# Grouped self attention of layer 0: the values become the weights of the product and stream four heads at once, with the normalisation on GpSimd ahead of it

## The chip, the cores and the metric

The program runs on one core of a Trainium2 chip. A core has five engines with queues of their own: TensorE (matmuls, with weight loads that overlap them), VectorE, ScalarE, GpSimd and SyncE, which here issues most DMAs. They meet only through semaphores. The metric is the time on the device of one execution, in microseconds; lower is better. In the rows of the profile PE is TensorE's matmul, PEld its weight load, DVE is VectorE, ACT is ScalarE, POOL is GpSimd, SP is SyncE.

## The reference

Two decoder layers over x of shape (8, 112, 512): B = 8 batches, T = 112 tokens, D = 512 features. Each layer has a self attention, a cross attention and a feed-forward block. Only one piece is touched, the attention inside `_L0_ffn_ref`: 32 query heads of 64 features share 8 key/value heads, 4 query heads each, with a causal mask.

```python
q = (h @ wq).reshape(B, S, NHEADS, HEAD_DIM)      # 32 heads of 64
k = (h @ wk).reshape(B, S, KVHEADS, HEAD_DIM)     # 8 heads of 64
v = (h @ wv).reshape(B, S, KVHEADS, HEAD_DIM)
q, k = _rope(q, k)
k, v = jnp.repeat(k, g, axis=2), jnp.repeat(v, g, axis=2)      # g = 4
scores = jnp.einsum('bqhd,bkhd->bhqk', q, k) / np.float32(np.sqrt(HEAD_DIM))
scores = jnp.where(causal[None, None], scores, jnp.float32(-1e+30))
attn = jax.nn.softmax(scores, -1)
o = jnp.einsum('bhqk,bkhd->bqhd', attn, v).reshape(B, S, NHEADS * HEAD_DIM)
x = x + o @ wo
h = _rms(x, ff_ln_w)
```

## The kernel before

The kernel is a chain of segments with one engine barrier between them. The one that matters is "self2". Its parts are written as generators, one for each engine; `attention_order` gives one list of turns, and `Segment.play` advances the named part by one turn on every engine. So each engine has a fixed order of instructions, and only semaphores tie the engines.

The attention part ("a", class `SelfAttentionPart`, L1466 to L1659) works on items. An item is one key/value head of one batch with its group of 4 query heads; two items (W = 2) make a step, so a batch has 4 steps and the segment 32, plus 2 to drain. Each step x has two turns, A and B:

- TensorE, A: transposes of the probabilities of pair x-2 (L1578, 8 of them, into the banks `t_banks`), then the scores of pair x (L1589, 8 matmuls with 64 rows; two items lie in the upper and the lower 64 rows). B: the value products of pair x-2 (L1602, 8 matmuls, the transposed probabilities as weights, 128 columns of the values streaming).
- VectorE, A: for each item the mask is added (L1618), reading the scores from PSUM and writing `p`; then the maximum of each row (L1622). B: for pair x-2 the reciprocal of the row sum (L1632) and the product into `o` (L1640). The row sum comes out of the value product itself: the value tile has a 65th column of ones for each head.
- GpSimd, A: the maximum is subtracted (L1565).
- ScalarE, A: copies of the transposes from PSUM (L1652). B: the exponential (L1656).

Here x-2 is counted on TensorE and ScalarE in steps, as LT = 2 and LE = 2. TensorE's transposes wait for `exp_done` of their item, the value products for `pt_ready`, the scores for `mask_done` of two items before.

The output part ("o", class `OutNormPart`, L2037 to L2285) works batch by batch, with 4 units of 512 columns: it turns a unit of `o` on TensorE (L2278, 4 transposes), ScalarE and VectorE split it into a high and a low half (L2127, L2179, tiles `oT_hi`, `oT_lo`), and TensorE multiplies by Wo (L2246, L2248, L2250, 12 matmuls of 512 columns for a unit). When a batch has its 4 units, VectorE adds and takes the moments (L2186 to L2151, the turn called ADD), GpSimd takes the power (L2118), VectorE scales (L2213, the turn NORM), and two turns later the result is turned (L2260) and split (L2130, L2167). With `gap=1.5` there are about two turns of "o" for three of "a": over four steps they stand after turn A of each step and once more after turn B of the third.

The part "w" (`WeightSplitPart`) splits Wo into halves in eight turns near the start (L2023 on ScalarE, L2031 on VectorE). `FirstBatchPart` (L2878) belongs to the segment before, "p2": it loads queries, keys and values of batch 0 ahead of time, the values in pieces of 64 into rows of 65, behind a memset of ones. `laid_out` is run on the host and only lays out the inputs.

The class `JointAttentionPart` of layer 1 (L1847 to L1998) is not changed, but the prediction reads prices there: its GpSimd normalises `p` before the transposes (L1920), and its value product has the values as weights and streams 448 columns (L1953).

Of the kernel before, what the change touches and what calls it, by code (L numbers as in the profile page):

```python
# [183 lines left out]
def reuse(eng, sem, value):  # L184

    if not isinstance(value, int) or value > 0:
        eng.wait_ge(sem, value)
# [1472 lines left out]


class CrossAttentionPart:

# [1214 lines left out]
class FirstBatchPart:  # L2878


    def __init__(self, g, name, p, loads, ones=None):
        landed, ones_set = g.sem(f"{name}_landed"), g.sem(f"{name}_ones_set")

        def sync(sp):
            yield
            n = 0
            for items, pairs in zip(((21,), (28,), (35,)), loads):
                sp.wait_ge(p.mm_done, TT)
                for i in items:
                    if i < 35:  # L2890
                        sp.wait_ge(p.t_stored[i % 3], 16 * (i // 3 + 1))
                    else:
                        sp.wait_ge(p.v_stored[0], 16)
                        if ones is not None:
                            sp.wait_ge(ones_set, 1)
                for to, src in pairs:
                    sp.dma_start(to, src).then_inc(landed, 16)
                    n += 16
                yield
            sp.wait_ge(landed, n)  # L2900

        def gpsimd(pool):
            yield
            if ones is not None:
                pool.wait_ge(p.mm_done, TT)
                pool.memset(ones, 1.0).then_inc(ones_set, 1)
            yield

        g.part(name, sync=sync, gpsimd=gpsimd)

# [442 lines left out]
def decoder(nc, ins, out, blocks=range(6), debug_x=None):  # L3353

    with ExitStack() as ctx:
# [8 lines left out]
        def tokens_of(b):  # L3364
            return slice(b * T, (b + 1) * T)

        def own_qkv(dh, heads, scale, *banks_and_mask):

            return (dh, None, lambda b: q_all[:, tokens_of(b)], lambda b: k_all[:, tokens_of(b)], lambda b: v_all[tokens_of(b), :],
                    heads, scale, *banks_and_mask)  # L3370

        def head_qkv(p):
# [63 lines left out]
        with hold_h0:  # L3436
            last_values = LastStores(core, hold_h0, "x2_last_values", [128, D])
            with ExitStack() as inner:
                cos_t = inner.enter_context(nc.sbuf_tensor("f0_cos", [128, TT, 2, 32], F32))
                sin_t = inner.enter_context(nc.sbuf_tensor("f0_sin", [128, TT, 2, 32], F32))  # L3440
                with Segment(core, "p2") as g:
# [4 lines left out]
                    k2 = first_hi[:, :, :].bitcast(F32).rearrange("p k d -> p (k d)")[:, 0:8 * T].rearrange("p (u c t) -> p u c t", u=2, c=4)  # L3446
                    v2 = first_lo[0:T, :, :].bitcast(F32).rearrange("p k d -> p (k d)")[:, 0:2 * (8 * 65 + 128)].rearrange("p (u e) -> p u e", u=2)
                    f = FirstBatchPart(g, "f", p, [
                        [(q2[0], q_all[:, tokens_of(0)].rearrange("(c p) t -> p c t", p=128))],
                        [(k2[:, 0, :, :], k_all[:, tokens_of(0)].rearrange("(c p) t -> p c t", p=128))],  # L3450
                        [(v2[:, 0, 0:8 * 65].rearrange("p (h e) -> p h e", e=65)[:, :, 0:64], v_all[tokens_of(0), :].rearrange("t (h d) -> t h d", d=64))]],
                        ones=v2)
                    order = ["p"] * 4 + ["p", "t", "t"] * (t.steps // 2)
                    g.run(f.placed(order + ["t"] * (t.steps - order.count("t")) + ["p"] * (p.steps - order.count("p"))))
            with Segment(core, "self2") as g:
                wo = [g.sb(f"wo_{part}", [128, 16, D], F32R) for part in ("hi", "lo")]
                a = SelfAttentionPart(g, "a", *own_qkv(64, 32, 0.125, (0, 1), (2, 3), (4, 5), "causal", ALU.add), tiles=(q2, k2, v2))
                w = WeightSplitPart(g, "w", "L0_ffn_wo", *wo)
# [100 lines left out]
def laid_out(inputs):  # L3559
# [18 lines left out]
    def pieces(w):  # L3578

        return rows_first(w).reshape(128, B, -1).transpose(1, 0, 2)  # L3580
# [13 lines left out]
    ins["L0_ffn_wk"], ins["L0_ffn_wv"] = rows_first(a["L0_ffn_wk"]), rows_first(a["L0_ffn_wv"])  # L3594
    ins["L0_ffn_wo"] = pieces(a["L0_ffn_wo"])
    ins["L0_ffn_wg"] = rows_first(a["L0_ffn_wg"])
# [48 lines left out]
```

## Time and profile before

| what | us |
|---|---|
| median of 3 runs | 2788.76 (2788.07 to 2790.92) |
| the profiled execution, its device time | 2790.01 |
| the profiled execution, its span | 2788.1 |
| TensorE busy in the span | 2570.0 (92%) |
| VectorE, ScalarE, GpSimd busy | 1694.7, 1132.2, 896.6 |
| segment "self2", first scores to last value product of it | 745.3 to about 972 |

The span runs from the first to the last instruction of the program. Busy time is a union over instructions; matmuls overlap, so a TensorE that is busy all the time may still have a little room. The granted clock is TensorE's, as a share of 2.4 GHz; its two levels are 1.00 and 0.50. In a timeline each line has start, duration (of a merged run, from the first start to the last end), engine, line of the program, tiles, count, and in brackets the idle time before it with what ended it.

### The profile page before, as it was taken

What the parts mean: (1) busy time and instruction counts of PE and PEld (TensorE: products, weight loads), DVE (VectorE), ACT (ScalarE), POOL (GpSimd) and SP (SyncE); (2) the same over time, 40 slices, a digit from 0 to 9 for tenths busy, and PEclk for the clock granted to TensorE, in tenths of its full rate; (3) what the DMA queues carried; (4) which work ended last, traced back from release to release, by engine and by line L of the source; (5) the groups of instructions that cost most, each with busy time, mean ns of one, the idle gap of its engine ahead of it and who ended that gap; (6) DMA issues with size and microseconds to landing.
All of it is one profiled execution on the core that took longest, in us unless ns stands there. A gap on an engine that the chain in (4) does not pass through costs nothing. (4 is left out here: it accounts for less than half of the span.)

```text
span 2788.1 us, 48182 instructions
## 1 busy us (share of the span) xinstructions
PE 2570.0 (92%) x14667; PEld 2065.4 (74%) x14668; DVE 1694.7 (61%) x3341; ACT 1132.2 (41%) x2434; POOL 896.6 (32%) x919
## 2 busy tenths in 40 slices
PE   8999799979899989799997898998999999899998
PEld 7888677768688877678875777774665678788887
DVE  4537757769776657567675566864434325666664
ACT  2113255533343324445453133755555522444443
POOL 3213100014332225423223200753333322345555
PEclk9999999999899979899998898999999989999999
DMA  5553122125532045388774432444222031566664
GB/s 188 154 144 99 31 92 63 59 66 154 162 104 64 15 142 172 123 235 224 193 213 120 112 73 70 131 132 149 73 64 73 22 128 55 154 163 161 162 153 81
DMA packets 289277, 332.87 MB, mean 119 GB/s; under 512 B 147445, under 2 KB 202693, under 8 KB 287312
## 3 DMA queue, kind: packets, MB, share of 16 engines
q1 hardware_dynamic: 217904, 252.57, 29.1%
q0 software_dynamic: 20640, 51.74, 9.6%
q10 hardware_dynamic: 50560, 26.34, 3.3%
q8 instruction: 99, 1.62, 0.2%
q14 instruction: 74, 0.61, 0.1%
HBM read 233.86 MB, written 96.72 MB: 119 GB/s over the span
## 5 line engine op out<-in xcount | busy, mean ns | idle before, releaser
L898 PE MATMUL e_psum<-e_up_hi,hT_hi 128*128 x672 | 245.2, 365 | 21.5 <-DVE hT_lo L867 14.6
L900 PE MATMUL e_psum<-e_up_hi,hT_lo 128*128 x672 | 236.7, 352 | 0.0
L899 PE MATMUL e_psum<-e_up_lo,hT_hi 128*128 x672 | 236.4, 352 | 0.0
L1920 POOL TENSOR_TENSOR joint_a_p<-joint_a_p,joint_a_rinv 112x487 f32<-112x487 f32 x128 | 125.2, 999 | 195.9 <-DVE joint_a_rinv L1966 195.5
L1565 POOL TENSOR_TENSOR self_a_p<-self_a_p,self_a_mx 112x448 f32<-112x448 f32 x96 | 96.0, 1000 | 205.2 <-DVE self_a_mx L1622 205.2
L898 PEld LDWEIGHTS e_psum<-e_up_hi,hT_hi 128*128 128x128 f32 x672 | 127.5, 190 | 43.6 <-issue 32.3
L1971 DVE TENSOR_REDUCE joint_a_mx<-joint_psum 112x1 f32<-112x487 f32 x128 | 85.0, 664 | 121.5 <-PE joint_psum L1941 121.2
L794 ACT ACTIVATE e_gate<-e_psum 128x352 f32<-128x352 f32 (+1 forms) x86 | 44.4, 516 | 256.4 <-PE e_psum L900 252.1
L873 DVE TENSOR_TENSOR hT_lo<-e_psum,hT_hi 128x256 fp32r<-128x256 f32 (+2 forms) x138 | 55.7, 435 | 142.1 <-ACT hT_hi L812 139.0
L1656 ACT ACTIVATE self_a_p<-self_a_p 112x448 f32<-112x448 f32 x128 | 71.6, 575 | 164.8 <-POOL self_a_p L1565 113.8
L900 PEld LDWEIGHTS e_psum<-e_up_hi,hT_lo 128*128 128x128 f32 x672 | 127.5, 190 | 11.5
L899 PEld LDWEIGHTS e_psum<-e_up_lo,hT_hi 128*128 128x128 f32 x672 | 127.7, 190 | 9.7
L1209 POOL TENSOR_TENSOR p_p_z<-p_p_straight,p_p_crossed 128x512 f32<-128x512 f32 x70 | 98.4, 1406 | 112.1 <-DVE p_p_crossed L1191 112.1
L828 DVE TENSOR_TENSOR e_up_lo<-e_up_raw,e_up_hi 128x1024 f32 (+3 forms) x128 | 128.0, 1051 | 3.2 <-issue 3.0
L766 POOL DMA_INDIRECT out<-e_y,e_back x51 | 123.2, 2416 | 17.3 <-issue 17.3
L847 DVE SCALAR_TENSOR_TENSOR e_act_raw<-e_gate,e_rows,e_psum 128x352 f32<-128x352 f32 (+1 forms) x86 | 55.4, 645 | 118.3 <-ACT e_gate L794 115.9
L898 PE MATMUL e_psum<-e_dn_hi,hT_hi 128*128 (+1 forms) x285 | 121.3, 426 | 1.0 <-issue 0.3
L1941 PE MATMUL joint_psum<-x_first,x_q 128*112 128x487 f32 x256 | 117.8, 582 | 1.8 <-PEq L89 1.7
L752 POOL TENSOR_TENSOR e_held<-e_zeros 1x1 f32<-1x1 f32 x90 | 19.7, 218 | 308.2 <-DVE e_idx L862 308.2
L142 PE MATMUL p_psum<-p_p_w_hi,hT_hi 128*128 128x512 f32 x280 | 115.5, 412 | 1.9 <-DVE p_p_w_lo L1175 1.9
L1994 ACT ACTIVATE joint_a_p<-joint_psum,joint_a_neg 112x487 f32<-112x487 f32 x128 | 85.4, 667 | 75.8 <-DVE joint_a_neg L1973 72.5
L781 ACT ACTIVATE e_up_hi<-e_up_raw 128x1024 f32 (+3 forms) x128 | 107.8, 923 | 15.1 <-PEq L89 15.1
(561 smaller groups left out, 7484.6 us busy)
## 6 DMA issues: line engine op xcount, KB each, us to landing
e_up_raw<-in_L_ffn_w SPq DMA_DIRECT2D x64, 512.0 KB, 4.8
e_up_raw<-in_L_ffn_w SPq DMA_DIRECT2D x64, 352.0 KB
e_dn_raw<-in_L_ffn_w SPq DMA_DIRECT2D x16, 1024.0 KB, 14.2
q_all<-p_p_t_stage ACTq DMA_DIRECT2D x56, 256.0 KB
e_dn_raw<-in_L_ffn_w SPq DMA_DIRECT2D x16, 512.0 KB
x_q<-q_all SPq DMA_DIRECT2D x8, 896.0 KB
v_ctx<-front_c_v_stage SPq DMA_DIRECT2D x24, 250.0 KB
x_others<-k_ctx SPq DMA_DIRECT2D x8, 750.0 KB, 4.6
```

The costliest lines, as they stand in the source:

```text
L142: last = pe.matmul(out, a, b, start=(k == 0 and i == 0), stop=(k == n_k - 1 and i == len(pairs) - 1))
L766: pool.indirect_dma_start(out=acc, out_offset=bass.IndirectOffsetOnAxis(ap=back[:, v, :], axis=0), in_=y[:, v, :], in_offset=None, compute ...
L781: act.activation(up_hi[:, bass.ds(slot * KC + k, 1), :], up_raw[:, k:k + 1, :], ACT.Copy).then_inc(up_hi_ready, 1)
L828: dve.tensor_tensor(up_lo[:, bass.ds(slot * KC + k, 1), :], up_raw[:, k:k + 1, :], up_hi[:, bass.ds(slot * KC + k, 1), :].bitcast(F32), AL ...
L898: pe.matmul(out, lhs[0], rhs[0], start=k == 0, stop=False)
L899: pe.matmul(out, lhs[0], rhs[1], start=False, stop=False)
L900: return pe.matmul(out, lhs[1], rhs[0], start=False, stop=k == n_k - 1)
L1209: both = pool.tensor_tensor(z[:, r, :], straight[:, r, :], crossed[:, r, :], ALU.add)
L1565: pool.tensor_tensor(p[:, i % RING, :, :], p[:, i % RING, :, :], mx[:, i % RING, :].unsqueeze(2).to_broadcast([T, group, T]), ALU.subtract ...
L1920: pool.tensor_tensor(p[:, r, :], p[:, r, :], rinv[:, r:r + 1].to_broadcast([T, S]), ALU.mult).then_inc(p_ready, 1)
L1941: pe.matmul(ps[0:T, s_banks[i % N_S], 0:S], q[:, b % 2, h, :], k[:, b % 2, h // group, :], start=True, stop=True).then_inc(s_done, 1)
L1994: act.activation(p[:, r, :], ps[0:T, s_banks[i % N_S], 0:S], ACT.Exp, bias=neg[:, r, :], scale=scale, accum_out=rsum[:, r:r + 1]).then_inc ...
```

## The change

A new class `GroupedSelfAttentionPart` takes the place of `SelfAttentionPart` in this one segment; the other two self attentions keep the old one. The steps, the two turns, the scores, the mask, the maximum, the subtraction, the exponential and the transposes stay. What differs:

- The value product. The weights are now the values of one key/value head (112 rows, 64 columns), and the transposed probabilities of the item's four heads stream as one block of 448 columns. The two items of a pair write the upper and the lower 64 partitions of one PSUM bank. 8 matmuls a pair become 2.
- Its result is feature-major. The output part reads it from PSUM with `ot_view` (`turned = True`), so `o`, the product into it (L1640) and the transposes L2278 are gone. Wo's rows are permuted on the host to the new order of heads.
- The row sum can't come from a column of ones any more. VectorE sums the rows of `p` of pair x-1 (L1794, a reduction for each item) in turn B, and takes one reciprocal for both items (L1798). GpSimd multiplies `p` by it in turn B (L1735). The transposes of pair x-2 wait for that product (`p_ready`), not for the exponential.
- The ring of transposed tiles `pt` has 4 places instead of 2; the values are loaded as plain rows of 512; `FirstBatchPart` loses the memset of ones.

Line numbers from L1655 on are those of the changed program here.

```diff
+        def gpsimd(pool):
...
+                for i in pair(step):
+                    pool.wait_ge(mx_ready, i + 1)
+                    pool.tensor_tensor(p[:, i % RING, :, :], p[:, i % RING, :, :], mx[...], ALU.subtract).then_inc(less_ready, 1)
+                yield
+                for i in pair(step, 1):
+                    pool.wait_ge(rinv_ready, i // W + 1)
+                    pool.tensor_tensor(p[:, i % RING, :, :], p[:, i % RING, :, :], rinv[...], ALU.mult).then_inc(p_ready, 1)
+                yield
+        def tensor(pe):
...
+                for i in pair(step, LT):
+                    pe.wait_ge(p_ready, i + 1)
+                    reuse(pe, pt_ready, i - N_T + 1)
+                    for j in range(group):
+                        last = pe.transpose(ps[0:T, t_banks[i % N_T], j * T:(j + 1) * T], p[:, i % RING, j, :], core.ident[0:T, 0:T])
+                    last.then_inc(t_done, 1)
...                                  # then the scores of the step, as before
+                yield
+                both = pair(step, LT)
+                if both:
...
+                    pe.wait_ge(pt_ready, both[-1] + 1)
+                    reuse(pe, self.o_used, at - N_O + 1)
+                    for i in both:
+                        n = i % n_items
+                        last = pe.matmul(ps[rows_of(i), o_banks[at % N_O], 0:group * T], v[:, b % 2, n * dh:(n + 1) * dh],
+                                         pt[:, i % PT, :, :].rearrange("p h t -> p (h t)"), start=True, stop=True)
+                    last.then_inc(pv_done, 1)
+        def vector(dve):
...                                  # mask and maximum of the step's pair, as before
+                yield
+                before = pair(step, 1)
+                for i in before:
+                    dve.wait_ge(exp_done, i + 1)
+                    dve.tensor_reduce(rsum[:, i % RING, :], p[:, i % RING, :, :], AX.X, ALU.add).then_inc(sum_ready, 1)
+                if before:
+                    at = before[0] % RING
+                    dve.wait_ge(sum_ready, before[-1] + 1)
+                    dve.reciprocal(rinv[:, at:at + W, :], rsum[:, at:at + W, :]).then_inc(rinv_ready, 1)
...
-                a = SelfAttentionPart(g, "a", *own_qkv(64, 32, 0.125, (0, 1), (2, 3), (4, 5), "causal", ALU.add), tiles=(q2, k2, v2))
+                a = GroupedSelfAttentionPart(g, "a", lambda b: q_all[:, tokens_of(b)], lambda b: k_all[:, tokens_of(b)], lambda b: v_all[tokens_of(b), :],
+                                             0.125, "causal", (0, 1), (2, 3), (4, 5), (q2, k2, v2))
...
-    ins["L0_ffn_wo"] = pieces(a["L0_ffn_wo"])
+    ins["L0_ffn_wo"] = pieces(a["L0_ffn_wo"].reshape(4, 2, 4, 64, D).transpose(0, 2, 1, 3, 4).reshape(4 * D, D))
```

How this stands on the engines. VectorE before, in the middle of the segment, from the second item's mask of one step on:

```order
L1618 TENSOR_TENSOR self_a_p<-self_psum,self_a_mask 112x448
L1622 TENSOR_REDUCE self_a_mx<-self_a_p 112x4
L2179 TENSOR_TENSOR self_o_oT_lo<-self_psum,self_o_oT_hi 128x448
L1632 RECIPROCAL self_a_rinv<-self_psum 112x4
L1640 TENSOR_TENSOR self_a_o<-self_psum,self_a_rinv 112x256
```

VectorE now, at the same place, to the end of the step (a step that also has the output part's split of the turned result):

```order
L1786 TENSOR_TENSOR self_a_p<-self_psum,self_a_mask 112x448
L1789 TENSOR_REDUCE self_a_mx<-self_a_p 112x4
L2336 TENSOR_TENSOR self_o_oT_lo<-self_psum,self_o_oT_hi 128x448
L1794 TENSOR_REDUCE self_a_rsum<-self_a_p 112x4 x2
L1798 RECIPROCAL self_a_rinv<-self_a_rsum 112x8
L2324 TENSOR_TENSOR hT_lo<-self_psum,hT_hi 128x4x112
```

The row sums of the pair before stand behind the mask and the maximum of this pair and behind the output part's turn; the reciprocal and the product of the finished pair are gone.

TensorE before, from the end of one output projection over the next step:

```order
L2248 MATMUL self_psum<-self_wo_lo,self_o_oT_hi 112x512
L2250 MATMUL self_psum<-self_wo_hi,self_o_oT_lo 112x512
L2278 MATMUL self_psum<-ident,self_a_o 128x112 x4
L1602 MATMUL self_psum<-x_first_lo,self_a_pt 112x128 x8
L1578 MATMUL self_psum<-ident,self_a_p 112x112 x8
L1589 MATMUL self_psum<-x_first_hi,x_wp_lo 112x112 x8
```

TensorE now, at the same place (L1747 are the transposes, L1758 the scores, L1772 the value products):

```order
L2405 MATMUL self_psum<-self_wo_lo,self_o_oT_hi 112x512
L2407 MATMUL self_psum<-self_wo_hi,self_o_oT_lo 112x512
L1772 MATMUL self_psum<-self_a_pt,x_first_lo 64x448 x2
L1747 MATMUL self_psum<-ident,self_a_p 112x112 x8
L1758 MATMUL self_psum<-x_first_hi,x_wp_lo 112x112 x8
```

The transposes still stand directly ahead of the scores; the turning of `o` is gone and the value products are 2 instead of 8.

## Rows read from the trace of the kernel before

**Rows 1.** Stretches of the segment: us, busy time by engine, PEclk, DMA share, GB/s.
```profile
745.30:788.00 42.70, 37.55 (x294) 32.43 (x294) 32.92 (x60) 23.53 (x37) 16.80 (x15) 0.82 0.61 174
788.00:954.30 166.30, 166.30 (x1369) 142.38 (x1368) 118.55 (x272) 62.90 (x129) 50.71 (x54) 1.00 0.19 51
```

**Rows 2.** Timeline of TensorE over one batch: start, duration, line, operands, count.
```profile
849.42 0.93 PE L1578 MATMUL self_psum<-ident,self_a_p 112*112 112x112 f32 x8
850.28 1.04 PE L1589 MATMUL self_psum<-x_first_hi,x_wp_hi 64*112 64x112 f32 x16
851.25 0.60 PE L2278 MATMUL self_psum<-ident,self_a_o 112*128 112x112 f32 x4
851.69 1.91 PE L1602 MATMUL self_psum<-x_first_lo,self_a_pt 112*112 112x128 f32 x16
853.44 0.93 PE L1578 MATMUL self_psum<-ident,self_a_p 112*112 112x112 f32 x8
854.30 1.04 PE L1589 MATMUL self_psum<-x_first_hi,x_wp_hi 64*112 64x112 f32 x16
...
861.15 1.04 PE L1589 MATMUL self_psum<-x_first_hi,x_wp_hi 64*112 64x112 f32 x16
...
871.17 1.04 PE L1589 MATMUL self_psum<-x_first_hi,x_wp_hi 64*112 64x112 f32 x16
```

**Rows 3.** Groups by line and shape, 788 to 954.3: busy, mean ns, idle before.
```profile
L1622 DVE TENSOR_REDUCE self_a_mx<-self_a_p 112x4 f32<-112x448 f32 x48 | 29.8, 621 | 1.6
L2213 DVE SCALAR_TENSOR_TENSOR self_w_raw<-h,self_o_rstd,self_o_w_row 112x512 f32<-112x512 f32 x6 | 4.5, 742 | 0.0
```

**Rows 4.** Timelines at the segment's start, TensorE, VectorE, GpSimd; low clock.
```profile
745.32 1.84 PE L1589 MATMUL self_psum<-x_first_hi,x_wp_hi 64*112 64x112 f32 x16 [5.16 <-PEq L89]
749.10 1.84 PE L1589 MATMUL self_psum<-x_first_hi,x_wp_hi 64*112 64x112 f32 x16 [1.95 <-DVE self_a_p L1618]
747.23 0.62 DVE L1618 TENSOR_TENSOR self_a_p<-self_psum,self_a_mask 112x448 f32<-112x448 f32 x1 [3.10 <-PE self_psum L1589]
747.89 0.62 DVE L1622 TENSOR_REDUCE self_a_mx<-self_a_p 112x4 f32<-112x448 f32 x1
748.43 0.61 DVE L1618 TENSOR_TENSOR self_a_p<-self_psum,self_a_mask 112x448 f32<-112x448 f32 x1
749.08 0.62 DVE L1622 TENSOR_REDUCE self_a_mx<-self_a_p 112x4 f32<-112x448 f32 x1
748.59 0.93 POOL L1565 TENSOR_TENSOR self_a_p<-self_a_p,self_a_mx 112x448 f32<-112x448 f32 x1 [2.76 <-DVE self_a_mx L1622]
```

**Rows 5.** Timeline of VectorE, an ADD turn of the output part.
```profile
961.05 0.68 DVE L2186 TENSOR_TENSOR h<-self_psum,h 112x512 f32<-112x512 f32 x1
...
963.64 0.61 DVE L2179 TENSOR_TENSOR self_o_oT_lo<-self_psum,self_o_oT_hi 128x448 fp32r<-128x448 f32 x1
964.17 0.17 DVE L1632 RECIPROCAL self_a_rinv<-self_psum 112x4 f32<-112x4 f32 x1
```

**Rows 6.** Timeline of the joint stage: value product, products on GpSimd, transposes.
```profile
1901.17 2.90 PE L1953 MATMUL joint_psum<-joint_a_pt,x_v 125*128 125x448 f32 x7 [2.01 <-ACT joint_a_pt L1988]
...
1909.42 1.96 POOL L1920 TENSOR_TENSOR joint_a_p<-joint_a_p,joint_a_rinv 112x487 f32<-112x487 f32 x2 [5.91 <-DVE joint_a_rinv L1966]
1910.47 2.12 PE L1933 MATMUL joint_psum<-ident,joint_a_p 112*125 112x112 f32 x8 [3.56 <-POOL joint_a_p L1920]
```

**Rows 7.** A wait of TensorE in the first self attention, and the clock of stretches.
```profile
340.15 1.01 PE L2260 MATMUL self_psum<-ident,self_p_w_raw 112*128 112x112 f32 x4 [5.83 <-DVE self_p_w_raw L2222]
340.20:347.20 7.00, 5.71 (x17) 4.84 (x18) 1.37 (x2) 0.54 (x1) 0.00 (x0) 0.50 0.00 0
745.30:760.20 14.90, 11.86 (x79) 10.78 (x80) 8.64 (x17) 6.65 (x11) 5.69 (x7) 0.50 0.72 192
```

**Rows 8.** Timeline of VectorE and GpSimd at a splitting step of Wo.
```profile
763.98 1.22 DVE L2031 TENSOR_TENSOR self_wo_lo<-self_w_raw,self_wo_hi 128x1024 fp32r<-128x1024 f32 x1
764.14 1.84 POOL L1565 TENSOR_TENSOR self_a_p<-self_a_p,self_a_mx 112x448 f32<-112x448 f32 x1 [0.25 <-DVE self_a_mx L1622]
```

**Rows 9.** DMA issues around the start of the segment: KB each, us to landing.
```profile
x_first_lo<-v_all SPq DMA_DIRECT2D x2, 224.0 KB, 4.5
```

More of the change, by code:

```diff
@@ L2878, with __init__ @@
 class FirstBatchPart:
-    def __init__(self, g, name, p, loads, ones=None):
-        landed, ones_set = g.sem(f"{name}_landed"), g.sem(f"{name}_ones_set")
+    def __init__(self, g, name, p, loads):
+        landed = g.sem(f"{name}_landed")
         def sync(sp):
@@ L2893, in sync @@
                         sp.wait_ge(p.v_stored[0], 16)
-                        if ones is not None:
-                            sp.wait_ge(ones_set, 1)
                 for to, src in pairs:
@@ L2900, in sync @@
             sp.wait_ge(landed, n)
[L2902 to L2909, printed above, removed]
+        g.part(name, sync=sync)
     def placed(self, order):
@@ L3365, in tokens_of @@
             return slice(b * T, (b + 1) * T)
-        def own_qkv(dh, heads, scale, *banks_and_mask):
-            return (dh, None, lambda b: q_all[:, tokens_of(b)], lambda b: k_all[:, tokens_of(b)], lambda b: v_all[tokens_of(b), :],
-                    heads, scale, *banks_and_mask)
         def head_qkv(p):
@@ L3446, in decoder @@
                     k2 = first_hi[:, :, :].bitcast(F32).rearrange("p k d -> p (k d)")[:, 0:8 * T].rearrange("p (u c t) -> p u c t", u=2, c=4)
-                    v2 = first_lo[0:T, :, :].bitcast(F32).rearrange("p k d -> p (k d)")[:, 0:2 * (8 * 65 + 128)].rearrange("p (u e) -> p u e", u=2)
+                    v2 = first_lo[0:T, :, :].bitcast(F32).rearrange("p k d -> p (k d)")[:, 0:2 * D].rearrange("p (u e) -> p u e", u=2)
                     f = FirstBatchPart(g, "f", p, [
@@ L3450, in decoder @@
                         [(k2[:, 0, :, :], k_all[:, tokens_of(0)].rearrange("(c p) t -> p c t", p=128))],
-                        [(v2[:, 0, 0:8 * 65].rearrange("p (h e) -> p h e", e=65)[:, :, 0:64], v_all[tokens_of(0), :].rearrange("t (h d) -> t h d", d=64))]],
-                        ones=v2)
+                        [(v2[:, 0, :], v_all[tokens_of(0), :])]])
                     order = ["p"] * 4 + ["p", "t", "t"] * (t.steps // 2)
```

105 lines of the change are left out of this document (added).

## The prediction, made before the changed kernel ran

> **What bounds the kernel now.** I read four views. The stretches first: inside the segment "self2" the middle 166.3 us have TensorE busy for all 166.30 us at granted clock 1.00, with VectorE at 118.55 and GpSimd at 50.71 [rows 1]; no stage outside this segment is touched. The timeline of TensorE next: the segment is 32 steps (8 batches x 4), each two items of four heads; from one score burst (L1589) to the next pass 4.02, 6.85, 10.02 and, in the fourth step as in the second, 6.85 us, 27.7 us for a batch [rows 2], and no idle time is noted between. Then the groups by line, for the price of one instruction [rows 3], and last the timelines at the segment's start, where engines do wait and the delay of each hand-over can be read [rows 4 to 6]. So today TensorE's own work sets the time, and everything else hides under it.
>
> **What TensorE loses in work.** For a pair of items the value products take 16 passes, 1.75 us from 851.69 to 853.44; the turning of the output (L2278) takes 0.44 us, 851.25 to 851.69 [rows 2]. After the change the pair's value product has four passes of 448 columns. By the 16 passes just named a pass costs 109 ns for 128 columns, so 0.38 for 448; the joint stage has passes of just this length, seven in 2.90 us with the last one's tail [rows 6], which agrees. One behind the other four make 1.52 us; if the two halves of the array run side by side, as the scores' two items do (16 passes of 112 columns in 0.97 us, 850.28 to 851.25, against 16 of 128 columns in 1.75 [rows 2]), three lengths or 1.14 us. L2278 goes. TensorE's work for a batch is then 27.7 - 4 x (0.42 + 0.23) = 25.1 us, or 23.6 with the halves side by side. The Trainium skill, "TensorEngine Tiling (Array Packing)", section "Theoretical Speedup", allows up to 2x for operands of at most 64 columns; by it the pair would cost 0.75 and the batch some 22 us. No row shows column halves at work, and the forecast below doesn't hang on it, since TensorE will no longer be what is waited for.
>
> **What the change adds, and where it lies.** Each item gets a row sum on VectorE and a normalising product on GpSimd before its transposes. The order that decides is this. In step x VectorE has mask and maximum of pair x (these need the scores of x), then the output part's work, then the row sums and reciprocal of pair x-1. GpSimd multiplies pair x-1 after that, TensorE turns pair x-1 after that, and only behind those transposes stand the scores of x+1. Before the change the transposes of x-1 waited for the exponential alone, long past. Now every step is one ring: scores x, VectorE, GpSimd, transposes x-1, scores x+1, and nothing in the ring can run ahead. I price it from the end of one score burst to the end of the next:
> - hand-over to VectorE 0.05 (the burst ends at 745.32 + 1.84 = 747.16, the mask starts at 747.23, at the low clock) [rows 4];
> - mask, maximum, mask, maximum: 747.23 to 749.08 + 0.62 = 749.70, 2.47 [rows 4];
> - one oT_lo of the output part, which stands between A and B turns in the order: 963.64 to 964.17, 0.53 [rows 5];
> - two row sums. They are not in the trace; the nearest row is the maximum over the same tile, 621 ns [rows 3], which advances the queue by about 0.54 (747.89 to 748.43) as other queued work does: 1.08. Bounds 1.0 to 1.3;
> - reciprocal 0.17 [rows 5] and its wait 0.03 (maximum behind its mask, 747.85 to 747.89 [rows 4]): 0.20; hand-over to GpSimd 0.08 (747.89 + 0.62 to 748.59) [rows 4];
> - two products over 112x448. The nearest row is the subtraction of the same shape, 0.93 undisturbed (748.59 [rows 4]); two queued ones overlap slightly (two of 487 columns take 1.96 [rows 6]): 1.82. Bounds 1.8 to 2.0;
> - GpSimd to TensorE 0.05 (first product 1909.42 + 1.00, transposes at 1910.47 [rows 6]), the second item's four transposes and the burst 1.52 (the eight start at 849.42, so the last four near 849.80; the burst ends at 850.28 + 1.04 = 851.32) [rows 2].
>
> Sum **7.80 us** for a plain step. In the step in which the output part adds a batch (ADD), seven more VectorE instructions stand ahead of the row sums: 961.05 to 963.64, 2.59 [rows 5], making 10.39. In the next one (NORM) one more of 742 ns [rows 3], 0.66 net: 8.46. The step with two output projections has TensorE as the slower: 10.02 - 0.4 - 0.23 to 0.61 = about 9.2. A batch: 7.80 + 10.39 + 8.46 + 9.2 = **35.85 us** against 27.73, +8.12. For the 6 batches of the middle stretch [rows 1]: **+48.7 us**.
>
> **The clock.** In the ADD step TensorE has only the value product (1.1 to 1.5) after the scores and then waits: the first product on GpSimd ends 0.05 + 2.47 + 2.59 + 0.53 + 1.08 + 0.20 + 0.08 + 0.93 later, 7.9, so some 6.5 us idle. The trace has one gap of that kind in the earlier self attention, 5.83 us ahead of 340.15, and the granted clock after it is 0.50 (1.2 instead of 2.4 GHz) for the 7.0 us from 340.20 [rows 7]. Four transposes and a burst at the low clock cost 0.32 + 0.80 more (burst 1.84 instead of 1.04 [rows 2, 4], four transposes 0.75 instead of 0.43), 1.2 us; the projection that follows slows down too, but hides under the ring (7.5 us of cover). 6 x 1.2 = **+7.2 us**. The Trainium skill, "TensorE: Matmul & The Clock Gate", section "HAM oscillation — how this bites in real kernels", says that waits between bursts make each burst start throttled; the row at 340.20 agrees. Without such a fall the total is 7 us less, and a fall that outlasts the projection is a rival below.
>
> **Head, tail, edge.** The first seven steps take 42.7 us now [rows 1], partly at the low clock. After: 3.8 (unchanged, bound by the mask, see the wait at 749.10 [rows 4]), then 7.80 - 0.53 + 1.2 = 8.5, then 9.4, three steps of 11.05, then 11. The last ones contain splitting steps of Wo: one ahead of the row sums (1.22 - 0.08 = 1.14) and one that keeps GpSimd from starting, as at 764.14 where a subtraction takes 1.84 instead of 0.93 while L2031 runs (+0.91) [rows 8]. Sum 65.9, **+23** (15 to 28). The tail exchanges a longer ring for less TensorE work, +1. Ahead of the segment the load of the values (4.5 us to land now, in pieces of 64 numbers [rows 9]) gets long pieces and loses its wait for the memset of ones: 0 to -2, I take -1. The permuted Wo and the value loads of later batches have the same bytes and lie under a queue that nobody waits for.
>
> Sum: 48.7 + 7.2 + 23 + 1 - 1 = **+79 us**. The profiled execution took 2790.0 us with a span of 2788.1, within 2 us of the median of 2788.76, so I add to the median: **2868 us**.
>
> **Rivals.**
> - *TensorE stays the bound.* If the ring were not closed (VectorE reaching the row sums of x-1 before it has to wait for scores x), TensorE's saving would be paid out: 0.65 to 1.0 us for each of 32 steps, 21 to 33 us, 2756 to 2768. It decides at 25 us a batch; the ring would have to shrink by 10. For it: TensorE's share of 1.00 and the idle quarter of VectorE. Against it: the order on VectorE, word for word. 7%.
> - *The low clock holds.* If the clock stays at 0.50 from the ADD step through the NORM step, projection (5.3), value product (2.3 to 3), transposes and scores (3.6) make the NORM step about 11.7 instead of 8.5 and cost some 3 more in the next: 7.4 instead of 1.2 a batch, +37 us, 2905. For it: from 745.3 to 760.2 the clock stayed at 0.50 with TensorE busy for 11.86 of 14.90 us [rows 7]. 15%.
> - *A shorter ring.* Overlap that I don't see (products of GpSimd running beside the sums, ADD work finding holes): 2 us less in each of 24 steps, 2800 to 2840. 10%.
> - *The halves don't run side by side.* Then only the step with two projections grows, by 0.2: no case of its own.
>
> **The numbers.** The forecast, a closed ring with one clock fall a batch, gets 66%, the low clock 15%, the shorter ring 10%, TensorE as the bound 7%, no change 2%. Own bounds of the ring (sums, products, head, no fall) give 2849 to 2885; the range takes in the shorter ring's upper edge and the low clock: **2840 to 2906**. A measurement of this kernel can tell 0.2% (6 us). Faster 7%, same 2%, slower 91%.
>
> **What would show it.** In the profile after: the mask's starts 7.8, 10.4, 8.5 and 9.2 apart instead of 4.0 to 10.0; TensorE waiting for GpSimd's product (L1735) at the transposes in three steps of four, 1.5 to 6.5 us; VectorE waiting for scores; TensorE's busy share in the middle near 70%; granted clock below 1.00 behind the ADD steps; row sums of 0.62 and products of 0.93. Wrong it would be if TensorE showed no gaps there, if the row sums of x-1 were seen ahead of the mask of x, or if GpSimd's product took far less than the subtraction.

## The result, and the profile after

The changed kernel takes **2888.08 us** (median of 4 runs, 2884.75 to 2891.72) against 2788.64 (2788.07 to 2790.92, 4 runs) for the kernel before: ratio 1.0354, 95% interval 1.0341 to 1.0367. It is slower by 99 us; 79 were forecast, in a range of 51 to 117.

The profile page of the changed kernel: span, busy time by engine, the granted clock in forty slices, and the group of the transposes with the wait ahead of it.

```profile
span 2890.0 us, 47097 instructions
...
PE 2579.8 (89%) x14155; PEld 2027.9 (70%) x14156; DVE 1701.4 (59%) x3309; ACT 1137.4 (39%) x2434; POOL 954.1 (33%) x982
...
PEclk9999899999788878989999799999999989999999
...
L1747 PE MATMUL self_psum<-ident,self_a_p 112*112 112x112 f32 x256 | 46.2, 325 | 91.5 <-POOL self_a_p L1735 91.5
```

Over the whole execution TensorE stands idle for 91.5 us ahead of the transposes (L1747), waiting for GpSimd's normalising product (L1735). The stretches of the segment, columns as in [rows 1]: its first seven steps, the next 24, its tail, and all that comes behind the segment.

```profile
745.20:810.60 65.40, 39.93 (x216) 26.85 (x217) 37.27 (x58) 24.27 (x38) 30.69 (x27) 0.65 0.37 114
810.60:1046.50 235.90, 171.76 (x985) 114.59 (x984) 122.36 (x247) 66.06 (x128) 94.47 (x102) 0.83 0.13 36
1046.50:1080.00 33.50, 24.82 (x114) 16.08 (x112) 14.87 (x32) 6.48 (x13) 7.05 (x8) 0.82 0.02 7
...
1080.00:2890.00 1810.00, 1664.87 (x8778) 1311.14 (x8776) 1045.93 (x1936) 790.69 (x1669) 668.81 (x706) 0.95 0.46 130
```

and, of the kernel before, its whole segment and what lies behind it:

```profile
983.10:2788.10 1805.00, 1663.56 (x8778) 1311.54 (x8776) 1046.05 (x1936) 789.82 (x1669) 672.46 (x706) 0.95 0.47 130
745.30:983.10 237.80, 228.46 (x1823) 195.25 (x1824) 167.14 (x368) 92.76 (x177) 70.47 (x73) 0.97 0.24 68
```

The same 24 steps that took 166.3 us with TensorE busy throughout [rows 1] take 235.9, and TensorE is busy for 171.8 of them, at a granted clock of 0.83 instead of 1.00. The spans differ by 101.9 us: head 65.4 - 42.7 = +22.7, middle 235.9 - 166.3 = +69.6, tail 33.5 - 28.8 = +4.7, behind the segment +5.0, ahead of it -0.1. What lies behind the segment has the same instructions (x8778 passes in both) and wanders from execution to execution: from the next segment's first matmul to the end it takes 1802.8 us in the trace before, 1807.8 in the changed kernel's, and between 1798.9 (e8) and 1810.4 (e2) in those of the experiments below, which don't touch it either. The 5 us lie inside that scatter, and the profiled execution of the changed kernel, 2891.72 us, is itself 3.6 above its median.

**The ring, row by row.** The timelines of the changed kernel for a plain step (a step without ADD, NORM or a second projection) and the ADD step behind it. Columns: start, duration, engine, line, operation, count, and in brackets the idle time ahead of it and who ended it. TensorE:

```profile
889.60 1.04 PE L1758 MATMUL self_psum<-x_first_hi,x_wp_lo 64*112 64x112 f32 x16
...
893.55 0.97 PE L1772 MATMUL self_psum<-self_a_pt,x_first_lo 112*64 112x448 f32 x4
896.02 0.59 PE L1747 MATMUL self_psum<-ident,self_a_p 112*112 112x112 f32 x4 [1.50 <-POOL self_a_p L1735]
896.91 0.66 PE L1747 MATMUL self_psum<-ident,self_a_p 112*112 112x112 f32 x4 [0.30 <-POOL self_a_p L1735]
897.50 1.84 PE L1758 MATMUL self_psum<-x_first_hi,x_wp_hi 64*112 64x112 f32 x16
899.27 1.68 PE L1772 MATMUL self_psum<-self_a_pt,x_first_lo 112*64 112x448 f32 x4
907.31 1.89 PE L1747 MATMUL self_psum<-ident,self_a_p 112*112 112x112 f32 x8 [6.36 <-POOL self_a_p L1735]
909.13 1.84 PE L1758 MATMUL self_psum<-x_first_hi,x_wp_hi 64*112 64x112 f32 x16
```

VectorE in the plain step:

```profile
890.67 0.62 DVE L1786 TENSOR_TENSOR self_a_p<-self_psum,self_a_mask 112x448 f32<-112x448 f32 x1 [0.53 <-PE self_psum L1758]
...
893.05 0.62 DVE L2336 TENSOR_TENSOR self_o_oT_lo<-self_psum,self_o_oT_hi 128x448 fp32r<-128x448 f32 x1
893.59 1.14 DVE L1794 TENSOR_REDUCE self_a_rsum<-self_a_p 112x4 f32<-112x448 f32 x2
894.75 0.20 DVE L1798 RECIPROCAL self_a_rinv<-self_a_rsum 112x8 f32<-112x8 f32 x1
899.37 0.62 DVE L1786 TENSOR_TENSOR self_a_p<-self_psum,self_a_mask 112x448 f32<-112x448 f32 x1 [4.41 <-PE self_psum L1758]
```

and GpSimd's products in the two steps:

```profile
895.04 1.82 POOL L1735 TENSOR_TENSOR self_a_p<-self_a_p,self_a_rinv 112x448 f32<-112x448 f32 x2 [0.89 <-DVE self_a_rinv L1798]
...
906.32 1.82 POOL L1735 TENSOR_TENSOR self_a_p<-self_a_p,self_a_rinv 112x448 f32<-112x448 f32 x2 [1.27 <-DVE self_a_rinv L1798]
```

Read it as a circle: scores end at 890.64, mask at 890.67, sums at 893.59, reciprocal at 894.75, products at 895.04, transposes at 896.02, next scores at 897.50; then VectorE, idle for 4.41 us, is released by those scores. In the ADD step the wait of TensorE is 6.36 us. From one burst to the next the 24 steps repeat four lengths: 7.84 to 7.97 us (plain), 10.83 or 11.45 to 11.63 (ADD), 9.3 to 9.7 (NORM), 8.96 to 11.59 (the step with two projections).

**The clock.** Stretches of the same kernel; the number ahead of the DMA share is the granted clock, 1.00 being 2.4 GHz and 0.50 being 1.2.

```profile
893.50:897.30 3.80, 2.00 (x13) 0.95 (x12) 1.42 (x4) 1.19 (x3) 2.47 (x3) 1.00 0.63 176
897.30:900.70 3.40, 3.40 (x23) 1.86 (x20) 1.29 (x3) 0.98 (x2) 0.00 (x0) 0.50 0.00 0
...
904.10:911.00 6.90, 3.69 (x25) 2.95 (x25) 2.08 (x7) 1.51 (x3) 2.37 (x3) 0.51 0.00 0
911.00:917.80 6.80, 4.46 (x20) 2.51 (x20) 4.84 (x9) 1.31 (x3) 4.08 (x4) 1.00 0.23 67
917.80:924.60 6.80, 6.69 (x30) 5.09 (x31) 3.83 (x7) 2.32 (x5) 1.92 (x3) 0.50 0.01 2
```

The clock falls three times in this batch: just behind the wait of 1.50 us of the plain step, within the 6.36 us of the ADD step, and behind a wait of 2.2 us in the NORM step (914.9 to 917.0), which leaves the step with two projections at half speed. In the 24 steps there are 14 such falls: six in ADD steps, three at the end of plain steps and five at the end of NORM steps.

### The profile page after: what moved, and what is told of

Same layout as the page of the kernel before. It is cut to its first block and busy times, and to the rows that moved or that the text cites. A ratio compares the mean times of both kernels' runs of the same rounds, so it can differ in the third digit from the quotient of the medians.

```text
span 2890.0 us, 47097 instructions
## 1 busy us (share of the span) xinstructions
PE 2579.8 (89%) x14155; PEld 2027.9 (70%) x14156; DVE 1701.4 (59%) x3309; ACT 1137.4 (39%) x2434; POOL 954.1 (33%) x982
## 3 DMA queue, kind: packets, MB, share of 16 engines
q8 instruction: 94, 1.54, 0.2%
## 5 line engine op out<-in xcount | busy, mean ns | idle before, releaser
L1747 PE MATMUL self_psum<-ident,self_a_p 112*112 112x112 f32 x256 | 46.2, 325 | 91.5 <-POOL self_a_p L1735 91.5
L766 POOL DMA_INDIRECT out<-e_y,e_back x51 | 113.6, 2227 | 16.4 <-issue 16.4
L1747 PEld LDWEIGHTS self_psum<-ident,self_a_p 112*112 112x112 f32 x256 | 31.5, 162 | 120.6 <-POOL self_a_p L1735 120.5
```

What stands on the lines that cost most here:

```text
L766: pool.indirect_dma_start(out=acc, out_offset=bass.IndirectOffsetOnAxis(ap=back[:, v, :], axis=0), in_=y[:, v, :], in_offset=None, compute ...
```

## The experiments

The theory: the steps are set by the ring, closed by the order on VectorE (row sums of pair x-1 behind the mask of pair x), and what the forecast missed is the clock. The rivals: the new instructions cost their own time wherever they stand; the excess over the forecast is longer steps and not the clock. Times of the kernel before beside these runs: 2792.04 us for e1 to e4, 2792.20 for e5 to e7, 2791.02 for e8, against 2788.64 beside the changed kernel. So a difference in us between two variants is good to some 3.5 us; the ratios go against the kernel before that ran beside each. In the diffs a line in round brackets stands for the lines named, moved as they are.

**e1_sums_first**, the order on VectorE alone.

```diff
             for step in range(n_all + LE):
+                (row sums and reciprocal of pair(step, 1))
                 for i in pair(step):
                     dve.wait_ge(s_done, i + 1)
                     ... mask, maximum
                 yield
-                (row sums and reciprocal of pair(step, 1))
                 yield
```

> The changed kernel, but VectorE takes the row sums and the reciprocal of pair x-1 ahead of the mask of pair x; GpSimd still has its product behind the subtraction of pair x. Theory of the closed ring: VectorE's sums (1.08 + 0.20), oT_lo (0.53) and the ADD and NORM work leave the ring, but the second maximum and the second subtraction stay in it. A plain step becomes 0.05 + 2.47 + 0.08 + 0.89 + 1.82 + 0.05 + 1.52 = 6.9 us, ADD the same, NORM 7.3 (the subtraction is held up while L2370 runs), the step with two projections 8.7 on TensorE: about 29.8 us a batch against 39 to 41 in the changed kernel and 27.7 before, so some 2805 us (2790 to 2825). Rival, the added work itself is the cost wherever it stands (VectorE and GpSimd busier): nothing is taken out, so 2880 to 2890. Rival, the low clock is the main cost: it goes only as far as the gaps go, 2850.

Measured 2847.99 us (2842.57 to 2852.40), ratio 1.0192 (1.0174 to 1.0210): 40 us of the 99 are gone, where 83 were expected (2805, in 2790 to 2825). The steps became 7.54 to 7.68 (plain), 9.5 to 10.3 (ADD), 8.15 (NORM), 8.97 us. VectorE and GpSimd in its ADD step say why it is so little. On VectorE the next pair's sums follow ADD's work at once:

```profile
884.43 1.14 DVE L1785 TENSOR_REDUCE self_a_rsum<-self_a_p 112x4 f32<-112x448 f32 x2
```

On GpSimd this pair's product starts only then:

```profile
884.06 0.55 POOL L2275 TENSOR_TENSOR self_o_rstd<-self_o_var_eps,self_o_expo 112x1 f32<-112x1 f32 x1 [1.66 <-DVE self_o_var_eps L2308]
884.58 1.82 POOL L1735 TENSOR_TENSOR self_a_p<-self_a_p,self_a_rinv 112x448 f32<-112x448 f32 x2
```

The reciprocal that the product at 884.58 needs was there since 876.06, but on GpSimd the product still stands behind the two subtractions of the step, which need the maxima, and in the ADD step behind the power (L2275), which needs all of VectorE's ADD work. The ring has a second closure, in GpSimd's order. My expectation had priced the second subtraction there, and neither ADD's work nor the power behind it. The middle of the segment, 24 steps:

```profile
801.10:1007.00 205.90, 160.70 (x985) 106.64 (x984) 121.68 (x244) 65.97 (x128) 93.54 (x102) 0.87 0.15 41
```

That is 30 us less than in the changed kernel, and not all of it is a shorter ring: the clock falls 7 times in these steps, instead of 14, and the step with two projections is 8.97 us in every batch. How much each is worth is not measured apart. The rival "the low clock is the main cost" had named 2850 us for this run, so this time by itself doesn't speak against it; e8 does.

**e5_product_first**, the order on GpSimd alone.

```diff
             for step in range(n_all + LE):
+                (products of pair(step, 1))
                 (subtractions of pair(step))
                 yield
-                (products of pair(step, 1))
                 yield
```

> Edit: on GpSimd alone, the two products of pair x-1 stand ahead of the two subtractions of pair x in every step; VectorE keeps its order (mask and maximum of pair x, then the row sums of pair x-1). Theory 1 (the ring closes through VectorE's queue: the sums of x-1 stand behind the mask of x, which needs the scores of x, which stand on TensorE behind the transposes of x-2): nothing is gained, since the products wait for sums that come no earlier; plain steps stay at 7.8 us, kernel 2880 to 2892 us. Theory 2 (GpSimd's own order holds the products back as well, independently): plain steps fall towards 6.9, kernel 2845 to 2870.

Measured 2882.67 us (2876.60 to 2884.13), ratio 1.0323 (1.0299 to 1.0347): nearly nothing gained, in theory 1's range. But the steps did not stay as it had them: the head became longer (steps of 11.8 us instead of 11.15) and the plain step is 8.45 in four batches of six instead of 7.84, because the subtractions now wait for the sums. GpSimd in one step:

```profile
901.78 1.82 POOL L1730 TENSOR_TENSOR self_a_p<-self_a_p,self_a_rinv 112x448 f32<-112x448 f32 x2 [6.82 <-DVE self_a_rinv L1798]
903.57 1.83 POOL L1734 TENSOR_TENSOR self_a_p<-self_a_p,self_a_mx 112x448 f32<-112x448 f32 x2
```

The products are first in the queue and stand idle for 6.82 us on the reciprocal. That the kernel is some 5 us faster all the same comes from the middle, 24 steps again:

```profile
809.60:1035.50 225.90, 161.02 (x987) 107.25 (x986) 121.78 (x246) 61.76 (x127) 90.75 (x104) 0.86 0.13 37
```

10 us less than 235.9, although no step is shorter than the ring makes it at full clock (7.84, 10.43, 8.50 and 8.96, by e8): the clock falls 7 times instead of 14, and the steps with two projections, up to 11.59 us before, are all 8.96.

**e2_open_ring**, both moves together.

> The changed kernel with both moves: VectorE's row sums and reciprocal of pair x-1 ahead of the mask of pair x, and GpSimd's product of pair x-1 ahead of the subtraction of pair x. Theory of the closed ring: now nothing between scores x and the product of x-1 depends on scores x, TensorE becomes the bound again with 27.7 - 4 x 0.42 (L2278) - 4 x 0.95 (value products, 0.8 us a pair in the changed kernel's trace) = 22.3 us a batch, plus one wait of some 1.5 us in the step with ADD: 24 us, 8 x 3.7 = 30 us under the kernel before, 2750 to 2765 us. Rival, added work as such: still near 2880. If only the order on VectorE mattered, it would equal the run with the sums alone moved, about 2805.

Measured 2782.92 us (2778.41 to 2790.61, 8 runs), ratio 0.9967 (0.9955 to 0.9979): 105 us less than the changed kernel, and 0.3% faster than the kernel before. The instructions are those of the changed kernel, with all row sums and products. That settles the main question: their own time is not the loss, their place in two queues is. One order alone gives 40 us, the other 5, the two together 105; each of the three contains clock falls that no longer happen (14 in the 24 middle steps of the changed kernel, 7, 7 and 1 in these).

It was still 18 to 33 us above what I expected. The segment, and then GpSimd from one pair's products to the next pair's:

```profile
745.00:976.20 231.20, 201.86 (x1311) 133.49 (x1312) 173.60 (x336) 91.82 (x177) 129.04 (x137) 0.93 0.25 70
```

```profile
900.79 1.83 POOL L1730 TENSOR_TENSOR self_a_p<-self_a_p,self_a_rinv 112x448 f32<-112x448 f32 x2 [4.04 <-DVE self_a_rinv L1789]
902.58 1.82 POOL L1734 TENSOR_TENSOR self_a_p<-self_a_p,self_a_mx 112x448 f32<-112x448 f32 x2
905.98 1.82 POOL L1730 TENSOR_TENSOR self_a_p<-self_a_p,self_a_rinv 112x448 f32<-112x448 f32 x2 [1.58 <-DVE self_a_rinv L1789]
```

Products, subtractions, exponentials, sums until 905.67, reciprocal at 905.70, products again: 900.79 to 905.98, a second ring of **5.19 us** that my expectation hadn't drawn. And in the ADD step VectorE has no gap from the reciprocal to the next one, 905.70 to 912.46; it is now what is waited for there:

```profile
905.70 0.20 DVE L1789 RECIPROCAL self_a_rinv<-self_a_rsum 112x8 f32<-112x8 f32 x1
...
911.29 1.13 DVE L1785 TENSOR_REDUCE self_a_rsum<-self_a_p 112x4 f32<-112x448 f32 x2
912.46 0.20 DVE L1789 RECIPROCAL self_a_rinv<-self_a_rsum 112x8 f32<-112x8 f32 x1
```

The scores of the four steps follow at 5.76, 3.74, 6.75 and 8.97 us, 25.2 a batch at full clock (before: 27.7), and the first seven steps take 50.7 us instead of 42.7. So of the 12.8 us gained in the middle (153.5 against 166.3) the head takes 8.

**e3_no_product**, GpSimd's product left out, so the division by the row sums is not made.

```diff
-                for i in pair(step, 1):
-                    pool.wait_ge(rinv_ready, i // W + 1)
-                    pool.tensor_tensor(p[...], p[...], rinv[...], ALU.mult).then_inc(p_ready, 1)
...
-                    pe.wait_ge(p_ready, i + 1)
+                    pe.wait_ge(exp_done, i + 1)
```

> The changed kernel without the normalising product on GpSimd: the transposes wait for the exponential, the row sums and reciprocals on VectorE are still computed but nobody uses them. Left out of the computation: the division by the row sums. Theory of the closed ring: there is no ring through VectorE's sums and GpSimd any more, TensorE sets the time: 22.3 to 23.5 us a batch, 2745 to 2760 us, and the row sums on VectorE cost nothing by themselves. Rival, VectorE's added sums are the cost: it stays above 2850.

Measured 2770.76 us (2769.22 to 2772.85), ratio 0.9918 (0.9902 to 0.9935), 11 us above the range I had given. The batch is 24.4 us (scores 5.8, 2.9, 6.8 and 8.97 apart) and the segment 213.9. This execution has the kernel's 64 products fewer, and it is only 12 us below e2: with the rings open the products, and e2's second ring with them, cost no more than that. What is left as a limit shows in one batch: TensorE is busy for 23.4 of its 24.4 us, VectorE for 20.2, and the one longer wait of TensorE, in the ADD step, is for VectorE:

```profile
812.40:836.80 24.40, 23.41 (x165) 15.83 (x164) 20.20 (x42) 10.47 (x22) 8.46 (x9) 1.00 0.24 67
```

```profile
871.86 0.46 PE L2399 MATMUL self_psum<-self_wo_hi,self_o_oT_hi 128*112 128x512 f32 x1 [0.90 <-DVE x_tok L2343]
```

**e4_fill, e6_more_fill, e8_fill_middle**: the changed kernel with small matmuls that nobody reads behind the value products, to keep TensorE busy where it waits. The ring is not touched.

```diff
                     last.then_inc(pv_done, 1)
+                fill = {0: 35, 1: 4, 3: 10}.get(step % n_steps, 0) if 7 < step < n_all else 0
+                for u in range(fill):
+                    pe.matmul(ps[0:T, t_banks[0], group * T:512], core.ident[0:T, 0:T], core.ident[0:T, 0:512 - group * T], start=True, stop=True)
                 yield
```

(e8; e4 has 30, 8, 6 and e6 36, 4, 6, both from step 3 on.)

> The changed kernel with small matmuls of 64 columns into unused columns of a transpose bank, placed on TensorE behind the value product in the steps where it waits (30 in the ADD step, 8 in the NORM step, 6 in the plain one); the ring is unchanged. Theory of ring plus clock falls: the steps become 7.84, 10.8, 8.5 and 8.9, 36 us a batch instead of 39.8, so 25 us less than the changed kernel, 2858 to 2868 us, at a granted clock near 1.00 in the middle of the segment. If the low clock were the main cost of the change, it would fall to 2800 or under. If the clock costs nothing because it hides under the ring, it stays at 2885 to 2890.

> The changed kernel with filler matmuls again: 36, 4 and 6 of them (e4_fill: 30, 8 and 6) behind the value products of the ADD, the NORM and the plain step. In e4_fill the 30 ran out 1.0 us before the transposes and the clock still fell once a batch. Theory 1 (the falls of the clock follow the idle stretches and cost what the half-speed passes on the ring take): no fall is left in the middle, the batch goes from 39.8 us in the changed kernel and 37.55 in e4_fill to 36.3 to 37.0, kernel 2865 to 2876 us. Theory 2 (what is above the forecast is not the clock but longer steps): the batch stays at 37.5 or more, kernel 2879 or more.

> The changed kernel with filler matmuls only from step 8 on: 35, 4 and 10 behind the value products of the ADD, the NORM and the plain step. In e6_more_fill the steps between falls of the clock were 7.84, 10.43, 8.5 and 8.97 us (35.74 a batch), but the filler ran in the head as well, there at half speed and in the way (one step of 18.6 us), and one fall a batch was left. Theory 1 (the whole excess of the middle over the forecast is the clock): the batch is 35.7 to 36.0 us with no fall, against 39.8 in the changed kernel, the head is that of the changed kernel, and the kernel takes 2862 to 2872 us. Theory 2 (the clock is the lesser part): 2876 us or more.

Measured: e4 2879.20 us (2874.26 to 2881.82), ratio 1.0306 (1.0288 to 1.0323); e6 2879.88 (2872.83 to 2884.11), 1.0309 (1.0285 to 1.0332); e8 2873.28 (2865.44 to 2876.29), 1.0299 (1.0280 to 1.0317). By total time e4 and e6 missed. In e4 the 30 ran out 1.0 us before the transposes, the clock still fell in each ADD step, and with 8 of them the NORM step takes 9.91 us, where the changed kernel has 9.3 to 9.7. In e6 the 24 middle steps take 222.2 us, but the filler also stood in the head, there at half speed, and made a step of 18.6 us out of 11.15:

```profile
777.98 13.70 PE L1777 MATMUL self_psum<-ident 112*112 112x64 f32 x72
```

e8 keeps it out of the head. Its 24 middle steps, then one batch of them (the step with two projections behind a wait of 1.2 us, then plain, ADD, NORM):

```profile
807.80:1030.00 222.20, 209.04 (x1555) 157.33 (x1554) 122.33 (x247) 65.87 (x128) 94.48 (x102) 0.96 0.14 38
871.90:882.50 10.60, 10.60 (x60) 7.57 (x58) 4.31 (x9) 2.83 (x6) 3.69 (x4) 0.84 0.01 2
882.50:890.30 7.80, 7.80 (x61) 5.76 (x60) 4.68 (x9) 2.69 (x6) 3.69 (x4) 1.00 0.58 147
890.30:900.70 10.40, 10.07 (x99) 8.78 (x98) 6.62 (x15) 2.77 (x6) 4.24 (x5) 1.00 0.01 2
900.70:909.20 8.50, 6.96 (x49) 4.69 (x48) 4.84 (x9) 2.66 (x5) 4.13 (x4) 1.00 0.18 54
```

With the clock up the steps are 7.84, 10.43 and 8.50 us, and 8.96 in the one batch that has no fall ahead of its step with two projections: **35.7 us**, against 35.85 forecast for the ring. The middle went from 235.9 to 222.2 us by matmuls that compute nothing, 13.7 us, and the median by 15 (2888.08 to 2873.28). The steps at full clock would make 6 x 35.72 = 214.3, so of the changed kernel's 235.9 some **21.6 us are clock**, 14 falls of 1.5 each in the mean. They are not equal. The six in the ADD steps cost 1.2 each, 0.4 in the step itself (10.83 for 10.43) and 0.8 in the next (9.30 for 8.50); the three at the end of plain steps some 0.8 each; and the five at the end of NORM steps, which leave the step with two projections at half speed, some 12 us together. In e8 five falls are left in six batches, each at the end of a NORM step behind a wait of 1.2 us, and cost 1.5 to 1.6 each: 214.3 + 5 x 1.5 is 221.8, for 222.2 measured. Theory 1 had expected no fall to be left, so the batch missed (37.3), while the time came out 1 us above its range.

**e7_split_between**, e2 with the eight splitting turns of Wo, one to a step and between its halves, in steps 0 to 7.

```diff
-for _ in range(min(len(extra), int(done_a >= extra_from and done_a % extra_gap == 0))):
+for _ in range(min(len(extra), int(done_a >= extra_from and done_a % extra_gap == extra_at))):
...
-extra=["w"] * 8 + ["gate"] * 3, extra_from=6))
+extra=["w"] * 8 + ["gate"] * 3, extra_gap=2, extra_from=1, extra_at=1))
```

> e2_open_ring (sums ahead of masks on VectorE, products ahead of subtractions on GpSimd) and, beside it, the eight turns that split the output weights into halves stand one to a step, between the two halves of steps 0 to 7, instead of one to a half step in steps 2 to 6. Theory 1 (in e2_open_ring the head is long, 50.7 us for seven steps against 42.7 in the kernel before, because the split that stands in the second half of a step waits for the exponentials of the step and holds up the sums that close the next one): the seven steps take 40 to 44 us, kernel 2772 to 2778 us. Theory 2 (the head is long because of the split's work itself, wherever it stands): kernel 2781 to 2785 us.

Measured 2785.74 us (2781.19 to 2787.37, 10 runs), ratio 0.9977 (0.9967 to 0.9987): no gain over e2. The head took 49.2 us instead of 50.7, with two steps of 6.65 us, and the eighth step was longer (10.95 for 6.10). Theory 1, with a head of 40 to 44 us, is wrong; theory 2's range ended 1 us below. GpSimd in one such step, with VectorE's split from 769.22 to 770.44 beside it:

```profile
767.03 1.82 POOL L1730 TENSOR_TENSOR self_a_p<-self_a_p,self_a_rinv 112x448 f32<-112x448 f32 x2 [1.58 <-DVE self_a_rinv L1789]
768.82 3.30 POOL L1734 TENSOR_TENSOR self_a_p<-self_a_p,self_a_mx 112x448 f32<-112x448 f32 x2
```

Two subtractions that take 1.82 us alone take 3.30 while VectorE splits: 1.5 us in the second ring, which is 6.65 instead of 5.19. In this place too the split costs its time on GpSimd.

## Why the prediction came out, step by step

- **What bounds.** Held. TensorE, busy for all of the middle before, is busy for 73% of it and waits for L1735 in three steps of four. None of the three signs that would have spoken against it is there: TensorE has the gaps, the row sums of x-1 stand behind the mask of x, and the product takes 0.93 us like the subtraction.
- **The ring, 7.80 / 10.39 / 8.46 / 9.2, a batch 35.85.** Held to 0.4%: 7.84, 10.43, 8.50, 8.96, together 35.7, at full clock (e8). The parts: hand-over 0.03 (0.05), mask and maximum twice 2.38 (2.47), oT_lo 0.54 (0.53), sums and reciprocal up to the products 1.45 (1.36), first product to transposes 0.98, the second 0.89 later. Pricing an absent row sum by the maximum of the same shape was right to 2% (609 against 621 ns), and an absent product by the subtraction to the ns where neither is disturbed (933). One reading was off: the hand-over in [rows 4] is 0.07 (747.16 to 747.23), not 0.05.
- **TensorE's work.** The value product was forecast at 1.14 to 1.52 us. It is 0.90 from its start to that of the next group (e2: 902.83 to 903.73), the first passes of its two halves starting 7 ns apart. The rule of up to 2x of the Trainium skill, "TensorEngine Tiling (Array Packing)", section "Theoretical Speedup", was nearer than my three lengths: the two pairs start 0.42 us apart, and four passes one behind the other, 0.42 each, would make 1.68 (an estimate; the joint stage's seven in 2.90 [rows 6] have 0.41 each). It changed nothing, as said, except in the step with two projections: 8.97 instead of 9.2.
- **The clock, 7.2 us.** This is the term that was mis-sized: 21.6 us. I allowed one fall a batch because I knew one gap (5.83 us, [rows 7]) and looked for gaps of that kind only (the trace has a second, 6.86 us ahead of 600.38). The fall in the ADD step is as described (6.3 to 7.1 us idle against 6.5 forecast, 1.2 us of cost; the prediction's own 0.32 + 0.80 makes 1.12, and its 1.2 is a slip that happens to hit), but there are falls behind waits of 1.5 and 2.2 us as well, and the one ahead of the step with two projections isn't hidden: there TensorE is the bound, and the step goes from 8.97 to as much as 11.6 us. The Trainium skill, "TensorE: Matmul & The Clock Gate", section "HAM oscillation — how this bites in real kernels", tells of a kernel in which each burst behind a wait for a DMA starts throttled. I applied that to the long wait alone; by the trace it holds for all six of the long ones, and the clock also falls behind three of six waits of 1.5 to 1.6 us in the plain step and five of six in the NORM step (0.9 to 2.2 us). The trace of the kernel before could have told: in its first self attention a wait of 1.14 us is followed by a fall.

```profile
267.50 1.04 PE L1589 MATMUL self_psum<-self_a_k,self_a_q 32*112 32x112 f32 x16 [1.14 <-DVE self_a_p L1618]
```

```profile
265.30:268.70 3.40, 2.20 (x28) 1.83 (x27) 3.26 (x9) 0.58 (x1) 2.09 (x3) 1.00 0.58 93
268.70:272.10 3.40, 3.40 (x9) 2.42 (x10) 3.19 (x9) 1.43 (x3) 0.32 (x1) 0.51 0.41 109
```

  The length of the wait doesn't decide by itself, though: in e5 the clock stayed at 1.00 behind four of five waits of 2.1 us. The rival "the low clock holds" described another thing, one long fall; the clock came back each time within 3.4 to 10.2 us.
- **Head, +23.** Held: the seven steps took 3.78, 8.51, 8.51, 11.10, 11.16, 11.15, 11.18 us, +22.7. The third was forecast at 9.4; the others are within 0.2.
- **Tail, +1.** It was 4.7: TensorE waits for L1735 twice more there (1.50 and 2.08 us), at a mean clock of 0.82.
- **Edge, -1.** The segment's first scores start at 745.21 ([rows 4]: 745.32), and between 741.9 and 746.3 in the experiments' traces. The load of the values takes 4.7 us to land (4.5 before). No gain is seen.
- **The sum.** 79 + 14.4 (clock) - 0.8 (ring) - 0.3 (head) + 3.7 (tail) + 1 (edge) + 5 (behind the segment) is 102, the difference of the spans. The forecast 2868 against 2888.08 is short by 20, and 14 of these are one term.
- **"TensorE stays the bound" was the right rival to name.** Its point of decision, the ring, is what e2 undoes. But opening VectorE's order alone, which I gave as its condition, opens less than half of it (e1), and with both opened the time is 2783, above the 2756 to 2768 that I gave for it, because of the longer head and the second ring.

## What to carry to other kernels

Before an operation is put between two engines that both work in program order, follow the next iteration's first instruction back through every queue; a ring that closes is priced as a sum of latencies, and it has to be opened in each queue that closes it, since one alone gives less than its share (40 and 5 us here, 105 together). Price what is not in the trace by the same shape on the same engine. And when TensorE changes from always busy to waiting, expect its clock to fall at some of the short waits too (here at waits from 1.1 us on), and count the falls ahead of those steps in which TensorE is itself the bound: five such falls cost 12 us, nine others 9.6.

## What the hardware showed that I had not expected

- The granted clock fell to 0.50 behind waits of TensorE of no more than 1.2 us (e8) and 1.5 us (changed kernel), but not behind every one of them. At half speed a score burst takes 1.84 us for 1.04 and the value product 1.68 for 0.97.
- Matmuls that compute nothing made the kernel 15 us faster (e8 against the changed kernel), and cost 7 us in a head where they themselves ran at half speed (e6: a step of 18.6 us for 11.15).
- Two products of 64 columns each into the two halves of the array ran fully beside each other: 0.90 us for four passes of 448 columns.
- VectorE and GpSimd slow each other where VectorE runs a split, an operation on two operands in SBUF. In the changed kernel's head a split on VectorE takes 1.54 us instead of 1.22 while two products on GpSimd take 2.81 instead of 1.82. Beside VectorE work with at most one operand in SBUF, the GpSimd operations of this shape keep to 0.93, all 54 of them in that trace:

```profile
795.64 2.81 POOL L1735 TENSOR_TENSOR self_a_p<-self_a_p,self_a_rinv 112x448 f32<-112x448 f32 x2 [1.11 <-DVE self_a_rinv L1798]
...
796.11 1.54 DVE L2188 TENSOR_TENSOR self_wo_lo<-self_w_raw,self_wo_hi 128x1024 fp32r<-128x1024 f32 x1 [0.55 <-ACT self_wo_hi L2180]
```

What stays open: whether any of the 5 us behind the segment belongs to the change; how the gains of e1 and e5 divide between ring and clock; what decides which of the short waits is followed by a fall; and how far e2 could go if its second ring and VectorE's ADD step were opened too. Its TensorE is busy for 23.9 of 25.2 us a batch, so with the same work on TensorE it could not be more than 1.3 us a batch there.
